# Loads moved into the last eight groups of one loop, and a late softplus moved behind the next group's products

## The reference, cut to what matters

```python
xn = _layernorm(x, gamma, beta)
x_inner, z = jnp.split(xn @ W_in, 2, axis=-1)                 # 512 channels each
x_conv = silu(causal depthwise conv of x_inner, width 4)
xp = x_conv @ W_x                                             # B (16), C (16) and one column for delta
delta = softplus(xp[:, :, -1:])
h_t = exp(delta_t * A) * h_{t-1} + delta_t * B_t * x_t        # per channel and state
y = (sum over n of h_t * C_t) + x_conv * D_skip
out = (y * silu(z)) @ W_out + residual
```

## Time and profile before

| | before |
|---|---|
| median of 3 runs | 1719.43 us (1718.05 to 1721.29) |
| profiled execution | 1721.67 us |
| its span | 1719.8 us |
| PE busy | 1648.0 us (96%) |
| DVE busy | 1303.9 us (76%) |
| ACT busy | 947.1 us (55%) |
| POOL busy | 871.4 us (51%) |
| DMA | 240.79 MB, mean 140 GB/s |
| first loop, from the trace | to about 252 us |
| second loop, from the trace | to about 520 us |

### The profile page before, as it was taken

One profiled execution on the slowest core, in us unless ns is written; L12 is line 12 of the kernel. 1 busy time (PEld: TensorE's weight loads), 2 busy tenths in 40 slices (PEclk: granted clock), 3 DMA queues, 4 the chain that ended last, 5 costly groups with the idle time before them and its releaser, 6 DMA issues.

```text
span 1719.8 us, 38082 instructions
## 1 busy us (share of the span) xinstructions
PE 1648.0 (96%) x11304; PEld 1492.5 (87%) x11305; DVE 1303.9 (76%) x2688; ACT 947.1 (55%) x1643; POOL 871.4 (51%) x770
## 2 busy tenths in 40 slices
PE   7999986999998999999999998999999999999994
PEld 6777765988987888888888878999999999999994
DVE  6888867888885776776776778767777777777774
ACT  6888876777843334334334345555555565555552
POOL 2111125888972345345345353555666666666664
PEclk9999988999998999999999999999999999999998
DMA  4555556899964343342342344334555455445454
GB/s 151 191 190 190 190 194 203 247 262 265 266 229 140 112 135 103 111 136 97 115 136 100 111 151 122 62 61 98 104 98 106 101 99 114 97 94 117 94 104 106
DMA packets 149263, 240.79 MB, mean 140 GB/s; under 512 B 40960, under 2 KB 104640, under 8 KB 141008
## 3 DMA queue, kind: packets, MB, share of 16 engines
q1 hardware_dynamic: 122608, 203.58, 38.1%
q0 software_dynamic: 26592, 36.46, 12.1%
HBM read 132.30 MB, written 107.68 MB: 140 GB/s over the span
## 4 chain that ended last, share of the span: by engine, by line
PE 62%; DMA 3%; DVE 2%; issue 1%; POOL 1%; ACT 0%; SPq 0%; DVEq 0%; ACTq 0%; POOLq 0%
PE block_banks L3094 22%; PE block_banks L3144 11%; PE block_banks L2976 5%; PE block_banks L2985 5%; PE block_banks L2899 4%; PE block_banks L2998 4%; PE block_banks L2920 2%; PE block_banks L3087 2%; PE block_banks L2939 2%; PE block_banks L2931 2%; PE block_banks L2887 1%; PE block_banks L2956 1%; DMA more<-back_y,back_token 1%; DMA attention_x<-x 1%; POOL sorted L2185 0%
## 5 line engine op out<-in xcount | busy, mean ns | idle before, releaser
L3094 PE MATMUL block_banks<-back_xe_T,back_w_split 128*128 128x256 f32 x3408 | 437.3, 285 | 2.4 <-DVE back_xe_T L2768 1.5
L3094 PEld LDWEIGHTS block_banks<-back_xe_T,back_w_split 128*128 128x128 f32 x3408 | 418.1, 192 | 2.8 <-issue 1.7
L2349 ACT ACTIVATE back_w_split<-back_w_gu 128x1024 fp32r x142 | 149.8, 1056 | 233.3 <-PE block_banks L3094 231.2
L3144 PE MATMUL block_banks<-back_w_down,back_he_T 128*128 x1680 | 213.1, 283 | 1.0 <-DVE back_w_down L2425 1.0
L3144 PEld LDWEIGHTS block_banks<-back_w_down,back_he_T 128*128 128x128 f32 x1680 | 206.6, 192 | 1.2 <-issue 1.2
L2748 DVE TENSOR_TENSOR back_w_split<-back_w_gu,back_w_split 128x1024 fp32r<-128x1024 f32 x142 | 179.6, 1265 | 36.9 <-ACT back_w_split L2349 36.7
L2185 POOL DMA_INDIRECT sorted<-back_x,back_slot x128 | 129.9, 1015 | 127.7 <-DVE back_slot L2571 80.5
L1582 PE MATMUL block_banks<-front_xn_T,front_w_in_parts 128*128 128x512 f32 x768 | 184.8, 395 | 2.4 <-DVE front_xn_T L1353 1.1
L1582 PEld LDWEIGHTS block_banks<-front_xn_T,front_w_in_parts 128*128 128x128 f32 x768 | 141.4, 188 | 39.2 <-DVE front_conv L1346 7.5
L2221 POOL DMA_INDIRECT acc<-back_y,back_token x71 | 112.3, 1581 | 120.5 <-DVE back_y L2787 116.2
L1346 DVE SCALAR_TENSOR_TENSOR front_conv<-block_banks,front_conv_wb,front_conv 128x508 f32<-128x508 f32 (+2 forms) x192 | 140.7, 740 | 33.0 <-ACT front_conv L1130 28.3
(11 more groups left out here) (290 smaller groups left out, 3492.0 us busy)
## 6 DMA issues: line engine op xcount, KB each, us to landing
back_xe<-sorted SPq DMA_DIRECT2D x72, 272.0 KB, 2.8
gate_T<-front_gate_T SPq DMA_DIRECT2D x16, 1024.0 KB, 4.8
xc_T<-front_xc_T SPq DMA_DIRECT2D x16, 1024.0 KB, 5.8
front_xc_in<-xc_T SPq DMA_DIRECT2D x16, 1024.0 KB, 7.4
front_gate_in<-gate_T SPq DMA_DIRECT2D x16, 1024.0 KB, 6.3
front_c_rep<-c_parts SPq DMA_DIRECT2D x128, 64.0 KB, 5.5
front_rows_in<-in_x SPq DMA_DIRECT2D x16, 512.0 KB, 8.2
x<-front_x SPq DMA_DIRECT2D x16, 512.0 KB, 3.1
```

What stands on the lines that cost most here:

```text
L2349: nc.scalar.activation(w_split[:, r, 0, m].unsqueeze(1), w_gu[:, bass.ds(e, 1), m], ACT.Copy).then_inc(w_high_ready, 1)
L3094: op = nc.tensor.matmul(dst[:, part, c % 2 * WINDOW:(c % 2 + 1) * WINDOW], w_split[:, r, w_part, m, k * D_FF + c * P:k * D_FF + (c + 1) * ...
L3144: op = nc.tensor.matmul(ps_y[:, s, 0:D_MODEL], he_T[:, r, h_part, k, seq(s)], w_down[:, bass.ds(e, 1), w_part, k], start=(n == 0), stop=(n ...
```

## The change

SP: `load_first` is gone. `load_sooner(g)` issues the same loads in pieces, behind the store of group g's gates, for g from 8 to 15; its waits are for stores of groups 0 and 1 and for things long done. The pairs 4 to 7 of SP's first loop are written out for it. Behind the first loop SP waits only for the stores of the first seven pairs; the wait for all of them stands in step 1. The store of delta moves from step 1 to step 14.

DVE: the last convolution of group 15 stands ahead of `delta_parts_of`. The ratio of the last eight sequences moves ahead of group 0's products. In step 0 the second half of group 0's skip stands behind the first multiply of group 1's products, and series, end, casts and steps behind the whole of those products.

TensorE: `segments` and the turning of delta move from step 0 into step 1, ahead of the out projection of group 0, with a wait there until ACT has copied both. The waits at the start of step 1 are gone. ACT: its two copies move from the end of step 0 to the end of step 1. The turned delta is in bank 4 instead of 3.

```diff
-            def load_first(u):
-                if u == 0:
+            def load_sooner(g):
+                if g == GROUPS - 8:
+                    sp.wait_ge(xc_stored[0], 32)
+                    load_xc(0, 0)
+                if g == GROUPS - 7:
+                    sp.wait_ge(gate_stored[0], 32)
+                    load_gate(0, 0)
+                if g == GROUPS - 6:
+                    load_rows(0, 0)
+                    sp.wait_ge(chain_step, W_STEPS)
+                    sp.wait_ge(xp_stored[0], 16 + 32)
+                    load_c(0, 0)
+                if g == GROUPS - 5:
                     sp.wait_ge(cleared, 3)
-                    sp.wait_ge(chain_step, W_STEPS)
-                sp.wait_ge(xp_stored[u], 16 + 32)
-                load_reps(u, u)
-                load_c(u, u)
-                sp.wait_ge(xc_stored[u], 32)
-                load_xc(u, u)
-                sp.wait_ge(gate_stored[u], 32)
-                load_gate(u, u)
-                load_rows(u, u)
+                    load_reps(0, 0, range(ENDS // 2))
+                if g == GROUPS - 4:
+                    load_reps(0, 0, range(ENDS // 2, ENDS))
+                    sp.wait_ge(xc_stored[1], 32)
+                    load_xc(1, 1)
+                if g == GROUPS - 3:
+                    sp.wait_ge(gate_stored[1], 32)
+                    load_gate(1, 1)
+                    load_rows(1, 1)
+                if g == GROUPS - 2:
+                    sp.wait_ge(xp_stored[1], 16 + 32)
+                    load_c(1, 1)
+                if g == GROUPS - 1:
+                    load_reps(1, 1)
...
@@ vector, last pair
                     if last and u:
+                        convolve(g, u, 3)
                         dve.wait_ge(chain_step, W_STEPS + RATIO + SERIES_POOL)
                         delta_parts_of(0, MOST)
-                    convolve(g, u, 3)
+                    else:
+                        convolve(g, u, 3)
@@ vector, step
-                if is_at(k, 0):
-                    softplus_series(MOST, SEQS)
...
-                if there(k):
+                if there(k) and not is_at(k, 0):
                     add_skip(k, u, 2)
-                if is_at(k, 0):
-                    softplus_end(MOST, SEQS)
-                    delta_parts_of(MOST, SEQS)
-                    all_steps(MOST, SEQS)
...
+                if is_at(k, -1):
+                    steps_by_pool()
+                    softplus_ratio(MOST, SEQS)
                 if there(k + 1):
...
                     nc.vector.tensor_tensor(inner, inner, of_b.unsqueeze(3).to_broadcast([P, GS, N, PART]),
                                             ALU.mult).then_inc(inner_cb, 1)
+                    if is_at(k, 0):
+                        add_skip(k, u, 2)
...
-                if is_at(k, -1):
-                    steps_by_pool()
-                    softplus_ratio(MOST, SEQS)
+                if is_at(k, 0):
+                    softplus_series(MOST, SEQS)
+                    softplus_end(MOST, SEQS)
+                    delta_parts_of(MOST, SEQS)
+                    all_steps(MOST, SEQS)
@@ tensor, step
-                if is_at(k, 1):
-                    pe.wait_ge(delta_rows_ready, 1)
...
+                if is_at(k, 1):
+                    pe.wait_ge(steps_ready, 2)
+                    pe.wait_ge(segment_ready, 2)
+                    segments(MOST, SEQS)
+                    pe.wait_ge(chain_step, W_STEPS + 2 * RATIO + SERIES_POOL + SERIES)
+                    nc.tensor.transpose(ps_delta, delta, ident).then_inc(delta_turned, 1)
+                    pe.wait_ge(segment_ready, 3)
+                    pe.wait_ge(delta_rows_ready, 1)
                 if there(k - 1):
...
-                if is_at(k, 0):
-                    pe.wait_ge(steps_ready, 2)
-                    pe.wait_ge(segment_ready, 2)
-                    segments(MOST, SEQS)
...
-                if is_at(k, 0):
-                    pe.wait_ge(chain_step, W_STEPS + 2 * RATIO + SERIES_POOL + SERIES)
-                    pe.wait_ge(skip_added, KI)
-                    nc.tensor.transpose(ps_delta, delta, ident).then_inc(delta_turned, 1)
```

More of the change, by code:

```diff
@@ L726, in decoder_front @@
         ps_out_last = ps[:, 0:2].rearrange("p a (b c) -> p (a b) c", b=2)
-        ps_count, ps_delta = ps[0:1, 2, 0:1], ps[0:SEQS, 3, 0:T]
+        ps_count, ps_delta = ps[0:1, 2, 0:1], ps[0:SEQS, 4, 0:T]
         weights_loaded = sem("weights_loaded")
@@ L900, in load_c, with load_reps @@
                                  d["c_reps"][g][:, c].partition_broadcast(PART)).then_inc(c_rep_loaded[u], 16)
-            def load_reps(g, u):
-                for c in range(ENDS):
+            def load_reps(g, u, ends=range(ENDS)):
+                for c in ends:
                     rows = slice(c * N, (c + 1) * N)
@@ L933, in body, with groups_stored @@
                         store_xp(g - 1, 1 - u)
-                    if last:
-                        load_first(u)
                     sp.wait_ge(gate_T_ready, KI * (g + 1) + 2)
                     sp.dma_start(d["gate_T"][g], gate_T[:, u]).then_inc(gate_stored[u], 16)
-            in_pairs(sp, body)
+                    if isinstance(g, int):
+                        load_sooner(g)
+            def groups_stored(pairs):
+                for stored, each in ((xc_stored, 16), (gate_stored, 16), (xp_stored, 32)):
+                    for u in range(2):
+                        sp.wait_ge(stored[u], each * pairs + 16)
+            body(0, False)
+            with sp.Fori(1, PAIRS - 4) as pair:
+                body(pair, False)
+            for pair in range(PAIRS - 4, PAIRS):
+                body(pair, pair == PAIRS - 1)
             store_xc(GROUPS - 1, 1)
             store_xp(GROUPS - 1, 1)
-            for stored, each in ((xc_stored, 16), (gate_stored, 16), (xp_stored, 32)):
-                for u in range(2):
-                    sp.wait_ge(stored[u], each * PAIRS + 16)
+            groups_stored(PAIRS - 1)
             same = None
@@ L953, in step @@
                 if is_at(k, 1):
+                    groups_stored(PAIRS)
+                if is_at(k, LAST_GROUP - 1):
                     sp.wait_ge(delta_rows_ready, 1)
                     sp.dma_start(d["delta"].rearrange("(b t) -> b t", b=SEQS), delta_rows).then_inc(delta_stored, 16)
-                if is_at(k, LAST_GROUP - 1):
                     sp.wait_ge(x1_stored[0], 32)
```

## The result

| | before | changed |
|---|---|---|
| median | 1719.35 us (22 runs) | 1722.70 us (22 runs) |
| ratio | | 1.0017, 95% interval 1.0010 to 1.0023 |
| profiled execution | 1721.67 us | 1720.77 us |
| its span | 1719.8 us | 1717.9 us |

So the change made the kernel 3 us slower, a little under the 0.2% that I had taken for the bound of no change. The forecast was 1711.6 us, with a range up to 1717.

The account below looks back on a forecast made before the run. The changeover was taken as bound by chains over DVE, ACT and POOL, the first loop and groups after 295.6 us by TensorE. 6.8 − 1.4 + 2.4 = 7.8 us gained gave 1711.6 us, range 1706 to 1717.

Parts of the forecast that it names:

- step 6: First loop, groups 8 to 15: loads in pieces ahead of `x_rows` lose 1.4 us, bounds 0 and 4.
- Step 1: Changeover: group 15's last convolution ahead of the casts; TensorE's 4.5 us wait falls to 1.1, everything behind 2.7 us earlier.
- Step 2: Changeover, DVE: the ratio ahead of group 0's products falls in a wait for ACT; nothing, at most 0.5 us lost.
- Step 3: Changeover, DVE: series, end, casts and steps leave the path to group 1's products, which end at 277.2, 7.2 us earlier.
- Step 4: Changeover, DVE: softplus's fourteen operations ahead of group 1's skip end at 282.0, 283.7 at worst; 1.8 us of waiting return.
- Step 5: Changeover: TensorE waits 1.8 us for ACT's copies; group 0's out matmuls start at 288.8, 6.8 us gained including step 1.
- Step 7: Second loop: SP loads sooner; group 2's 1.1 us `xc_in` wait goes, and 2.4 of the later 5.3 us.
- The clock rival: TensorE's clock falls again: `apply(1, 0)` costs 1.8 us more, half the out matmuls 3.5 more; time 1717, chance 0.14.
- The slower rival: First loop, groups 11 to 15: `x_rows` behind a megabyte lands late, 8.1 us more; time 1719.7, chance 0.05.

Follow-up runs that it names:

- e1_behind_x: Against the changed kernel, all early load pieces stand behind the same group's `x_rows` load; 1711.15 us, ratio 0.9956 to the kernel before.
- e1_again: Second run of the kernel with all pieces behind `x_rows`; 1712.55 us against 1719.14 for the kernel before, ratio 0.9969.
- f1_copies_first: All pieces behind `x_rows`, plus segments, turned delta and ACT's two small copies moved earlier in step 1; 1712.56 us, ratio 0.9963 to the kernel before.

## Why the prediction was wrong, step by step

**The step that failed is 6**, the cost of the pieces in the first loop: 1.4 us in the sum, with a bound of 4; the trace has 9.9, which is also the prediction's own sign of being wrong (a first loop longer by over 4 us). With the pieces behind `x_rows` the loss was gone. The mechanism stood in the step, and again as the rival on the slower side; its size was wrong in three terms.

- *A megabyte ahead.* For groups 8 and 9 I took 2.6 us more, the time of the bytes alone. The `x_rows` behind group 8's piece landed 9.0 us after its issue instead of 5.6, so 3.4 later. The margin was bare: DVE waited 0.84 and 0.90 us, and TensorE lost 1.5, where I had 0.2 for both.
- *Eight small loads.* I gave group 10's piece nothing, and wrote that it makes it by 0.5 to 2 us. My own rows said otherwise: with 3.7 us for the eight issues and 5.7 to land, as I reckoned for group 12, `x_rows` is 1.4 us late here too. Then the issues took 4.89 us, and the landing 5.9. DVE waited 2.7 us, and TensorE lost 2.6. Group 12's eight small loads took 4.9 us as well (208.54 to 213.43). So its `x_rows` was issued 1.2 us later than forecast against its own gate store, and it landed in 7.7 us instead of 5.7: a wait of 4.3 us where I had 1.4.
- *The clock.* I priced each wait at its own length. Behind the longest the granted clock fell to the lower level and the next 24 matmuls took 1.6 us more; in the kernel with small pieces ahead, a wait of 1.84 us cost 3.7.

The chance was mis-set with it. I gave 0.05 to the case that the first loop pays, because the old loads landed 2.5 us before they were read. But 2.5 us is less than the 3.7 us of issue that two of the pieces put in front: the argument spoke for the rival.

**The rest of the sum was nearly right, and some 2 us too high.** Without the loss of step 6 it gives 9.2 us; the kernel with the pieces behind `x_rows` gained 7.5 and 6.6. With 9.9 in place of 1.4 it gives a loss of 0.7 us, where the changed kernel lost 3.3. So that kernel's 1711.15 and 1712.55 us, close to the 1711.6 forecast for the changed one, are no hit: that forecast has the 1.4 us of loss in it.

Point by point, the other steps. Where nothing else is said, the places are those of `e1_behind_x`, whose first loop is as long as the old one:

- *Step 1* was right. The big step product starts at 248.45 (forecast 248.6), TensorE's segments at 249.68, and its wait for the silu is 1.1 us as forecast.
- *Step 2* stood at the edge of its bound. In the changed kernel two of the five instructions took 1.1 and 1.2 us beside POOL, and the products came late by it; TensorE first waited 2.8 us for ACT's masks all the same, and then 0.55 us for the products, where I had at most 0.5.
- *Step 3* was right: the products end at 276.1 (forecast 277.2).
- *Step 4* was right in size. The series took 4.63 us instead of 3.09, and the fourteen instructions ended at 281.9 (forecast 282.0). Eight instructions of 0.17 us each would take 1.4, so some 3.3 us were blocked, near the 3.4 of my worst case. The six behind them ran free, at 0.17 to 0.28 us each: POOL's last multiply beside the series ended at 279.7. By the Trainium skill, SBUF — State Buffer, section Who interferes with whom, a DVE instruction with two SBUF inputs and a GpSimd one that reads SBUF exclude each other; the trace agrees for the series.

```profile
276.06 4.63 DVE L1451 SCALAR_TENSOR_TENSOR front_soft<-front_soft 128x8 f32<-128x8 f32 x8
```

- *Step 5* came out in its sum, by terms that cancel: the out matmuls start at 289.25, and at 289.61 in `e1_again` (forecast 288.8). The low clock, which I had said would go with the old waits, stayed, and `apply(1, 0)` took 3.62 and 3.10 us where I had 1.95. Against that, in the first of the two the products came 1.1 us sooner and the wait ahead of `apply(1, 2)` was 0.5 us (forecast 1.8), with 2.5 us for ACT at the end (1.8); in the second the two waits were 1.4 and 1.6. `f1_copies_first` shows that the last wait was set by the order of work on ACT.
- *Step 7* was right in its amount, and its cause is not shown. The five later waits of 5.3 us became four of 3.3 in the changed kernel, and group 2's wait of 1.1 us went, as forecast. But the later waits came to only 2.0 us in the kernel with the new order of work alone, whose loads are not early. What made them shorter stays open.
- *The clock rival* came in by its first half: `apply(1, 0)` took 3.41 us in the changed kernel and 3.62 with the pieces behind. This window of the latter has a granted clock of 0.50. The out matmuls took 7.14 us in both, as at full clock.

```profile
276.00:280.00 4.00, 3.80 (x16) 3.59 (x17) 3.86 (x6) 1.63 (x2) 3.67 (x3) 0.50 0.50 156
```

- *The slower rival* is what happened. Its text adds 8.1 us to the 1.4 for three groups with a megabyte ahead, so 9.5, and the trace has 9.9. That the two are so near is luck in part: the three groups lost 0.6, 0.9 and 5.8 us where it had 2.7 more in each, and group 10, with no megabyte load ahead, had the second largest loss.

What stays open: the changed kernel's median is 3.3 us above that of the kernel before, while the two traces reach attention at the same point. The new trace is of an execution 2 us below its median, the old one of one 2 us above, which is enough for the gap; no run says where in the kernel it arises.

## What to carry to other kernels

Before a transfer is put into a loop that has room for it, find the next load that the loop itself needs, and its margin from landing to reading; here 2.5 us. What is put ahead of it in the same queue costs its issue time and its landing time behind what is already there, not the time of its bytes alone; here the same bytes, put behind that load, cost the first loop nothing.

And when two edits each remove what the other waits for, neither may show a gain alone, as here; a run of each alone still tells which one carries a loss.

## What the runs showed of the hardware

- Eight loads of 64 KB took SP 3.71 us to issue behind nothing but small loads, and 4.89 us when a store of 1 MB and a load of 512 KB had been issued within 1 us before them.
- A load of 512 KB landed 5.6 us after its issue behind a store of 1 MB, and 9.0 us when a load of 1 MB stood between the two.
- A wait of TensorE of 1.84 us, in a loop that was otherwise full, was followed by a low clock (0.64 over 4 us, 24 matmuls in 7.33 us); one of 2.32 us in the changed kernel, ahead of the row at 192.74 above, was not (24 in 5.75 us). How long a wait is does not tell by itself whether the level falls.
